# A fused two-layer graph transformer on one core: the second layer's work moved one group later, with its x2 turned over by way of DRAM

## The reference

```python
# layer 0 (8 heads of 32)
nx = ln(x, ln1_g, ln1_b)
q, k, v = heads(nx @ wq + bq), heads(nx @ wk + bk), heads(nx @ wv + bv)
scores = q @ k.T / sqrt(32) + where(adj > 0, 0.1 * adj * adj, -inf)
x1 = x + (softmax(scores) @ v) @ wo + bo
x2 = x1 + gelu(ln(x1, ln2_g, ln2_b) @ w1 + b1) @ w2 + b2      # hidden size 1024
# layer 1 (one head of 256)
sc = where(adj == 0, -inf, (x2 @ Wq) @ (x2 @ Wk).T / sqrt(256))
y = x2 + (softmax(sc) @ (x2 @ Wv)) @ Wo + bo
out = layer_norm(y) * gamma + beta
```

## Time and profile before

| | |
|---|---|
| time, median of 3 | 890.98 us (890.16 to 891.61) |
| profiled execution | 891.15 us, its span 889.4 us |
| PE busy | 853.3 us (96%) |
| PEld busy | 754.3 us (85%) |
| DVE busy | 703.3 us (79%) |
| ACT busy | 609.6 us (69%) |
| POOL busy | 507.5 us (57%) |
| DMA moved | 107.32 MB, mean 121 GB/s |
| mean granted TensorE clock | 0.983 |

### The profile page before, as it was taken

One profiled execution on the slowest core, in us unless ns is written; L12 is line 12 of the kernel. 1 busy time (PEld: TensorE's weight loads), 2 busy tenths in 40 slices (PEclk: granted clock), 3 DMA queues, 4 the chain that ended last, 5 costly groups with the idle time before them and its releaser, 6 DMA issues.

```text
span 889.4 us, 21938 instructions
## 1 busy us (share of the span) xinstructions
PE 853.3 (96%) x7059; PEld 754.3 (85%) x7059; DVE 703.3 (79%) x2548; ACT 609.6 (69%) x1830; POOL 507.5 (57%) x374
## 2 busy tenths in 40 slices
PE   8899797799999999999999999999999999999996
PEld 8787687589898989889898988989798988989795
DVE  6695777868888898888888797888889887875636
ACT  5684865667868676776768676786867677684542
POOL 3522743756666565775647566666656577655312
PEclk9899999799999999999999999999999999999998
DMA  8000245445536353444546343553635343343001
GB/s 272 16 24 13 66 105 187 129 152 136 177 94 200 101 180 99 127 154 114 181 118 189 106 146 105 138 176 95 200 96 182 86 124 120 99 143 115 24 1 36
DMA packets 131122, 107.32 MB, mean 121 GB/s; under 512 B 5750, under 2 KB 112908, under 8 KB 131084
## 3 DMA queue, kind: packets, MB, share of 16 engines
q1 hardware_dynamic: 131068, 106.85, 40.5%
q10 hardware_dynamic: 16, 0.00, 0.0%
HBM read 61.48 MB, written 45.35 MB: 120 GB/s over the span
## 4 chain that ended last, share of the span: by engine, by line
PE 74%; ACT 3%; DVE 3%; POOL 1%; issue 1%; DVEq 0%; POOLq 0%
PE bank L455 21%; PE bank L457 20%; PE bank L456 20%; PE bank L618 3%; PE bank L743 3%; PE bank L774 3%; PE bank L642 3%; ACT p L1116 2%; PE bank L724 1%; DVE p L1540 1%; PE bank L767 0%; POOL p_s L2013 0%; POOL x_bo L1983 0%; POOL x_b L1993 0%; DVE stats L1375 0%
## 5 line engine op out<-in xcount | busy, mean ns | idle before, releaser
L1052 ACT ACTIVATE p_s<-bank,neg_max 128x128 f32<-128x128 f32 x464 | 163.0, 391 | 78.2 <-DVE neg_max L1443 78.1
L2013 POOL TENSOR_TENSOR p_s<-p_s,rsum 128x512 f32<-128x512 f32 x116 | 118.1, 1041 | 73.9 <-DVE rsum L1450 52.2
L455 PE MATMUL bank<-w_hi,hT_hi 128*128 128x256 f32 x512 | 147.5, 288 | 1.3 <-DVE hT_lo L1316 1.3
L457 PE MATMUL bank<-w_hi,hT_lo 128*128 128x256 f32 x512 | 144.1, 281 | 0.0
L456 PE MATMUL bank<-w_lo,hT_hi 128*128 128x256 f32 x512 | 144.0, 281 | 0.0
L1443 DVE CUSTOM_DVE_ANT_0 bank<-bank,bias 128x128 f32<-128x128 f32 x464 | 117.4, 325 | 2.0 <-PE bank L618 1.5
L455 PE MATMUL bank<-n2T_hi,w_hi 128*128 128x512 f32 (+1 forms) x272 | 111.4, 409 | 5.1 <-DVE hT_lo L1316 5.1
L1083 ACT ACTIVATE bank<-bank,vec_cols 128x512 f32<-128x512 f32 (+1 forms) x136 | 86.5, 636 | 31.1 <-PE bank L457 22.5
L1052 ACT ACTIVATION_READ_ACCUMULATOR p_s<-bank,neg_max 128x1 f32 x464 | 107.1, 231 | 0.0
L456 PE MATMUL bank<-n2T_lo,w_hi 128*128 128x512 f32 (+1 forms) x272 | 105.2, 387 | 0.0
L457 PE MATMUL bank<-n2T_hi,w_lo 128*128 128x512 f32 (+1 forms) x272 | 105.1, 387 | 0.0
(11 more groups left out here) (242 smaller groups left out, 2432.6 us busy)
## 6 DMA issues: line engine op xcount, KB each, us to landing
parked<-pT SPq DMA_DIRECT2D x116, 256.0 KB, 3.8
pT<-parked SPq DMA_DIRECT2D x15, 1024.0 KB, 5.5
p_s<-parked SPq DMA_DIRECT2D x14, 1024.0 KB, 7.7
xs<-in_x SPq DMA_DIRECT2D x15, 512.0 KB, 3.9
out<-y SPq DMA_DIRECT2D x14, 512.0 KB, 3.0
x_bo<-in_x SPq DMA_DIRECT2D x13, 512.0 KB, 3.8
parked_x<-nx SPq DMA_DIRECT2D x48, 128.0 KB, 2.5
hT_hi<-parked_x SPq DMA_DIRECT2D x12, 512.0 KB, 5.0
```

Of the source, the lines that this page charges most:

```text
L455: mm(out, a_hi, b_hi, start=first, stop=False)
L457: return mm(out, a_lo, b_hi, start=False, stop=last)
L1052: last = run(to, of, ACT.Exp, scale=-1.0, bias=neg_max[:, r, place:place + 1], accum_out=psum[:, r, place:place + 1])
L2013: P.tensor_tensor(p_s[:, r, :, :], p_s[:, r, :, :], rsum[:, r, :, None].to_broadcast([128, 4, NODES]), ALU.mult).then_inc(pool_p, 1)
```

## The change

Layer 1 of a group is made one turn later. A turn has a new name `gl = gp - 3` for the group of layer 1, and `gc` becomes `gp - 4`. Turn 4 has neither (`None`). `last_turn` makes layer 1 of group 14 among the up-projections of group 15. `late(g)` is true for groups 2 to 14.

For these groups x2 is no longer transposed by TensorE: VectorE transposes blocks of x2 into x1_b2's place (`x2blocks`), SP stores them (`store_x2T`, four DMAs of 128 KB) and loads them (`load_x2T`, one DMA of 512 KB); in the next turn ScalarE makes the high part (`landed_high`) and VectorE the low part (`x2T_low`). x2 plus bo1 is stored to DRAM (`store_x2`, 512 KB) and loaded into y's place (`load_y`, 512 KB); `residual3` adds to it there. The mask of layer 1 is made from a second load of the adjacency (`load_adj1`, 256 KB, `mask_landed`), and `move_up` is gone from the turns. On TensorE the q-k product stands ahead of the values of gp, and the scores ahead of both value-output products.

```diff
 SP
+            def load_x2T(g):
+                sp.wait_ge(x2T_store, 64 * g - 64)
+                sp.wait_ge(pe_s1, g)
+                sp.dma_start(x2T_f[:, :, :], parked_x2T[g].rearrange("t c j a b i -> (c j) t (a b i)")).then_inc(x2T_load, 16)
+            def load_y(g):
+                sp.wait_ge(x2_store, 16 * g - 16)
+                sp.wait_ge(out_store, 16 * g)
+                sp.dma_start(y[:, :, :].rearrange("p b d -> p (b d)"), parked_x2[g]).then_inc(y_load, 16)
...
-            def turn(gp, gc):
+            def turn(gp, gb, gl, gc):
...
                     load_adj(gp + 1)
-                store(gc)
+                load_adj1(gb)
+                if gc is not None:
+                    store(gc)
                 store_blocks(gp, 0)
+                if gl is not None:
+                    load_y(gl)
                 if not is_last(gp):
                     load_nx(gp + 1)
+                store_x2T(gb)
                 load_xbo(gp)
                 if not is_last(gp):
                     store_blocks(gp, 1)
+                load_x2T(gb)
                 for q in pairs(gp):
                     load_blocks(gp, q)
+                store_x2(gb)
 TensorE
@@ n2_transpose
-                    pe.wait_ge(act_t, g)
-                    pe.wait_ge(dve_t, g)
-                    pe.wait_ge(dve_s1, g)
+                    done = g if opening(g, 3) else g - 1
+                    pe.wait_ge(act_t, done)
+                    pe.wait_ge(dve_t, done)
+                    pe.wait_ge(dve_s1, done)
@@ turn
                 mlp_down(gb, 0)
+                if gl is None:
+                    out_project(ga, 0)
                 mlp_down(gb, 1, (0,))
                 if size(gp) > 2:
                     scores(gp, 1)
+                if gl is None:
+                    out_project(ga, 1)
+                    mlp_down(gb, 1, (1,))
+                    project_v(gp, 0)
+                    n2_transpose(ga, True)
+                    project_v(gp, 1)
+                    return
                 mlp_down(gb, 1, (1,))
                 out_project(ga, 0)
-                x2_transpose(gb)
                 out_project(ga, 1)
+                t_project(gl)
                 project_v(gp, 0)
-                t_project(gb)
-                vo_project(gb, 0, True)
-                scores1(gb)
-                vo_project(gb, 1, True)
+                scores1(gl)
+                vo_project(gl, 0, True)
+                vo_project(gl, 1, True)
                 n2_transpose(ga, True)
-                p1_transpose(gb)
+                p1_transpose(gl)
@@ last_turn
-                for j in range(4):
-                    mlp_up(gb, j, True)
+                mlp_up(gb, 0, True)
+                mlp_up(gb, 1, True)
+                t_project(gl)
+                mlp_up(gb, 2, True)
+                mlp_up(gb, 3, True)
+                scores1(gl)
+                vo_project(gl, 0, False)
+                attend(ga, 0)
                 mlp_up(gb, 4, True)
-                attend(ga, 0)
+                vo_project(gl, 1, False)
                 mlp_up(gb, 5, True)
                 mlp_up(gb, 6, True)
+                pe.wait_ge(dve_vo, gl)
                 out_project(ga, 0)
                 mlp_up(gb, 7, True)
+                p1_transpose(gl)
                 mlp_down(gb, 0)
+                attend1_pairs(gl)
+                mlp_down(gb, 1, (0,))
                 n2_transpose(ga, False)
-                mlp_down(gb, 1)
+                mlp_down(gb, 1, (1,))
 ScalarE
+            def landed_high(g):
+                act.wait_ge(x2T_load, 16 * g - 16)
+                act.wait_ge(pe_vo, pair0(g))
+                for t in range(KT):
+                    identity(nx_split(x2T[0], g, t), x2_landed(g, t)).then_inc(act_x2T_hi, 1)
@@ turn
                 nx_high(gp)
+                if gl is not None:
+                    landed_high(gl)
                 for j in range(4):
                     gelu(gb, j)
...
                 if whole:
-                    exps(gp, 1, 0)
-                    exps(gp, 1, 1)
-                for t in range(KT):
-                    x2T_copy(gb, (t,))
-                    x2T_high(gb, (t,))
-                if whole:
-                    exps(gp, 1, 2)
-                    exps(gp, 1, 3)
+                    for r in range(HPT):
+                        exps(gp, 1, r)
+                if gl is not None:
+                    t_copy(gl)
                 v_copy(gp, 0)
-                t_copy(gb)
-                vo_copy(gb)
-                exps1(gb)
+                if gl is not None:
+                    vo_copy(gl)
+                    exps1(gl)
@@ last_turn: landed_high(gl) ahead of the GELUs; between GELU 5 and 6 a probe for Exp, exps1(gl), a probe for Gelu
 VectorE
+            def x2blocks(g):
+                dve.wait_ge(dve_x2, pair0(g) + 2)
+                turned = flat(x1_b2[:, :, :]).rearrange("p (t c b i) -> p t b c i", t=KT, c=4, b=PER)
+                for t in range(KT):
+                    V.transpose(turned[:, t], x2[:, :, 128 * t:128 * t + 128].rearrange(
+                        "p b (c j) -> p b c j", c=4)).then_inc(dve_x2blocks, 1)
@@ x2T_low
+                    if late(g):
+                        V.tensor_tensor(nx_split(x2T[1], g, t), x2_landed(g, t), nx_split(x2T[0], g, t).bitcast(f32),
+                                        ALU.subtract).then_inc(dve_x2T, 1)
+                        continue
@@ turn
-                norm3(gc)
+                if gc is not None:
+                    norm3(gc)
+                if gl is not None:
+                    x2T_low(gl)
                 attn_low(ga, 0)
...
                 residual1(ga, 0, True)
-                x2T_low(gb)
+                x2blocks(gb)
                 residual1(ga, 1, True)
                 sums2(ga, 0)
+                if gl is not None:
+                    t_copy(gl)
                 sums2(ga, 1)
...
                     blocks(gp, 1, 0)
-                t_copy(gb)
...
-                biased1(gb)
+                if gl is not None:
+                    biased1(gl)
...
-                vo_copy(gb)
+                if gl is not None:
+                    vo_copy(gl)
...
-                inverse_sums1(gb)
-                residual3(gb, 0)
-                residual3(gb, 1)
+                if gl is not None:
+                    inverse_sums1(gl)
+                    residual3(gl, 0)
+                    residual3(gl, 1)
 GpSimd
+            def mask_landed(g):
+                k = size(g)
+                pool.wait_ge(adj1_load, 16 * g - 16)
+                pool.wait_ge(dve_s1, g)
+                pool.sem_inc(stand_pool, 1)
+                P.tensor_copy(pen1[:, 0:k, :], adj_w[:, 0:k, :]).then_inc(pool_adj_f, 1)
...
+                P.tensor_scalar(pen1[:, 0:k, :], pen1[:, 0:k, :], 0.0, MASKED, ALU.is_equal, ALU.mult).then_inc(pool_pen1, 1)
@@ first_turn: move_up(2) is gone; second_turn: mask1(2) and move_up(3) are gone
@@ turn
                 for r in range(HPT):
                     normal(gp, 0, r)
-                x2_plus_bo(gb)
...
                 if size(gp) > 2:
                     normal(gp, 1, 3)
+                x2_plus_bo(gb)
                 x_plus_bo(gp)
                 x1_plus_b2(ga)
-                mask1(ga)
-                move_up(gp)
+                mask_landed(gb)
```

More of the change, by code:

```diff
@@ L54, in is_last, with late, opening @@
     return isinstance(g, int) and g == GROUPS - 1
+def late(g):
+    return not (isinstance(g, int) and (g < 2 or g > GROUPS - 3))
+def opening(g, first):
+    return isinstance(g, int) and g < first
 def toks(g):
@@ L590, in project_v @@
                 elif not (isinstance(g, int) and g < 3):
-                    pe.wait_ge(*((dve_x1, pair0(g) - 1), (dve_vo, g - 2))[q])
+                    pe.wait_ge(*((dve_x1, pair0(g) - 1), (dve_vo, 1 if opening(g, 4) else g - 3))[q])
+                    if q == 1 and not opening(g, 4):
+                        pe.wait_ge(dve_x1, pair0(g))
                 for b in (2 * q, 2 * q + 1):
@@ L730, in t_project @@
                     pe.wait_ge(dve_s1, g)
+                elif isinstance(g, int) and g == GROUPS - 3:
+                    pe.wait_ge(act_p, 4 * pair0(g + 2) + 4)
+                elif late(g):
+                    pe.wait_ge(dve_x2, pair0(g + 2))
                 for m in range(KT):
@@ L742, in scores1 @@
                     for t in range(KT):
-                        last = mm(bank[at("s1", g)][:, nodes(b)], home("tT", g)[:, t, nodes(b)], home("x2T_f", g)[:, t, nodes(b)],
+                        x = x2_landed(g, t)[:, b] if late(g) else home("x2T_f", g)[:, t, nodes(b)]
+                        last = mm(bank[at("s1", g)][:, nodes(b)], home("tT", g)[:, t, nodes(b)], x,
                                   start=(t == 0), stop=(t == KT - 1))
@@ L1554, in residual3 @@
                     dve.wait_ge(dve_r1, g + 1)
-                    dve.wait_ge(pool_x2b, g + 1)
-                    if not is_last(g):
```

(28 more changed lines are left out.)

204 lines of the change are left out of this document (138 added, 66 removed).

## The result

The changed kernel takes 942.05 us (median of 5 runs, 941.21 to 944.40), the kernel before 891.18 us beside it. The ratio is 1.058, its 95% interval 1.0565 to 1.0592: slower by 51 us. The forecast was 946 in a range of 905 to 961.

A forecast was written before the change was run, and what follows sets the result against it. TensorE's queue of work was taken to bound the kernel. Eleven turns of 3.0 + 0.5 + 0.5 = 4.0 us make 44, the ends 11.3, together 55.3 on 891.15 us: 946, range 905 to 961.

The forecast's parts named there:

- The head: Start of a turn: late x2T load delays ScalarE's first GELU and TensorE's up-projections, +3.0 us a turn.
- The clock: TensorE's granted clock falls behind new waits of 2.3 and 1 us: between 0 and 1.7 us a turn, 0.5 taken.
- Rival C: The clock falls in every turn at the full price, 11 x 1.2 us more, 959; chance 0.06.
- The tail: End of a turn: VectorE's masked scores hold back TensorE's relief and a GpSimd lock delays VectorE, +0.5 us a turn.
- a tail without a lock: Tail if VectorE's x2T low copies don't contend with GpSimd's gain: n2 slightly earlier, -0.15 us a turn.
- the first runs, then the gain, then the second: Behind norm3, GpSimd's 2.38 us gain runs between VectorE's two x2T low copies, making VectorE 1.65 us late at avT_lo.
- 3.0 + 0.5 + 0.5: Price of turns 5 to 15: late load at the start, VectorE's chain at the end, slower clock; 4.0 us a turn.
- The ends: Second turn -0.9, turn 4 -2.0 and +1.0 clock, turn 5 +1.7, last turn +10, turn 16 +1.5: 11.3 us.
- B: Faster: TensorE's relief of 1.1 us a turn arrives if masked scores and load are in time, 885; chance 0.06.
- A: x2T load lands in time or its wait is absorbed; 0.6 head and 0.5 tail a turn, 913; chance 0.16.
- D: Neither cost nor gain: delays and relief are taken up in VectorE's idle fifth, 891; chance 0.02.

The follow-up runs named there:

- Experiments 1 to 3: Changed kernel with one edit each: x2T load ahead of stores, 899.56 us; high copies behind GELUs, 899.27 us; key projections between fourth and fifth up-projection, 908.50 us.
- kernel 1: Changed kernel with the load of x2T issued on SP ahead of the four stores of the second half of the blocks: 899.56 us, ratio 1.0105.
- Experiments 4 to 7: Old tail order on the changed kernel, 929.72 us; with early load, 889.24; with early load, only VectorE's tT copy moved, 895.54, only TensorE's and ScalarE's order, 921.67.
- kernels 5 and 11: Changed kernel with early x2T load and old tail order, 889.24 us; the same plus key projections after the fourth up-projection and turn 4's chain brought forward, 885.73 us.
- kernel 5: Changed kernel with both repairs, the x2T load ahead of the block stores and the old order in the tail: 889.24 us, ratio 0.9997.
- kernel 4: Changed kernel with the old tail order on TensorE, ScalarE and VectorE, the x2T load left late: 929.72 us, ratio 1.0448.
- kernel 7: Changed kernel with early x2T load and the old order on TensorE and ScalarE, VectorE's tT copy kept between the statistics: 921.67 us, ratio 1.0364.

## Why the prediction held, and where it did not

**The head.** The mechanism is as forecast, and each step of it: issue at the turn's start, landing at +5.1 (forecast +4.7), ScalarE's GELU late, fifth up-projection at +8.32 (+8.1). Experiments 1 to 3 show it from three sides. The size of the wait was 2.5 us a turn, not 3.0: the eighth up-projection did not wait for VectorE at +13.05, since the slow clock brought TensorE there only at +14.2 by itself. Taking the late load away gives back 37.3 us in ten turns, 3.73 a turn; I had 3.0 and a share of the clock.

**The clock.** Too small: 0.5 forecast, 1.38 measured. Rival C's mechanism, a fall in every turn, was the true one: each of the ten turns has a mean granted clock of 0.97. It did not give 959 since the head and the tail were cheaper.

**The tail.** This term failed: +0.5 forecast, -0.1 measured. TensorE has 1.12 us a turn less to do (507.91 us in before's ten turns, 496.67 in kernel 1) and waits 1.02 us ahead of n2. That is close to the -0.15 that the prediction gave for a tail without a lock. In kernel 1 the 0.2 us left in the head take up the rest, so its period is before's (50.86 against 50.87).

The step that failed is "the first runs, then the gain, then the second", which put +0.65 on the tail. x2T's low copies took 1.28 us together, not over 2, and GpSimd's gain gave way, 3.35 us instead of the 2.38 of the earlier trace rows:

```profile
452.94 1.28 DVE L1654 TENSOR_TENSOR x2T_lo<-x2T_f,x2T_hi 128x512 fp32r<-128x512 f32 x2
455.36 0.69 DVE L1431 TENSOR_TENSOR avT_lo<-bank,avT_hi 128x512 fp32r<-128x512 f32 x1 [1.14 <-ACT avT_hi L1082]
...
453.10 3.35 POOL L2173 TENSOR_TENSOR y<-y,gamma_r 128x1024 f32<-128x1024 f32 x1 [1.61 <-DVE y L1507]
```

VectorE still waits 1.14 us behind it, so nothing is late. That one of the two stands still while the other works is what the Trainium skill states in "SBUF — State Buffer", section "Who interferes with whom", and this row agrees with it (3.35 is 2.38 and about what was left of the pair). The same section gives the ports to the one that issues first; by that GpSimd, from 453.10 on, would have gone ahead of VectorE's second copy, as the prediction had it, and the row shows otherwise.

The rest of the tail held as forecast: the statistics end at 476.47 and the masked scores begin at 480.84, 4.4 us later (4.5), and TensorE idles 1.02 us ahead of n2 (1.0). What the prediction did not ask is whether the relief could be had by another order. Experiments 4 to 7 show that the wait came from the new order. Without it 0.88 of the 1.1 us arrives.

**What adds up.** By TensorE's own rows, per steady turn: wait in the head +2.52, wait ahead of n2 +1.02, clock +1.38, less work -1.12, and 0.08 that it idled before: +3.72, measured +3.71. The forecast was 3.0 + 0.5 + 0.5. Terms of opposite sign made 40 for ten turns and 37.1 measured look closer than its parts were; that is luck.

By the kernels: the late load +3.73, the order +0.87, the delay by a group with both repaired -0.88. These are differences along one row of kernels, so that they add up is no test. Taken the other way round, the old order is worth 1.37 (kernel 4) and the early load 3.23. The two overlap by 0.5 us, most of it the clock.

**The ends.** Turn 4 -2.05 (forecast -1.0), turn 5 +3.03 (+5.7), turn 16 +3.49 (+1.5: the clock fell there too, 0.97), the last turn +11.20 (+10), in kernels 5 and 11 +9.8: TensorE's added work, busy 67.97 us after 56.98. Up to turn 4 it was -2.8 where I had -0.9; most of this is the scatter of the opening, and the second turn itself gave 0.5. So about 2 of the 5 us by which the total of 50.0 is under the 55.3 are scatter.

**Rivals.** B's point was at VectorE's masked scores and the load, and kernel 5 shows it to be the right one: with both in time TensorE's relief arrives. But B's -13 us for 12 turns was too much, it is 0.88 a turn, so with the ends even a repaired change is even with before. A (load in time, 913) has kernel 1 as its test: 900, because its 0.5 us in the tail are not there, and its 0.6 in the head are 0.35, which the relief pays for. D is out.

**Open.** The mean price of the clock is 0.92 us a turn behind the wait in the head alone (kernel 4: 506.23 us of work, kernel 5 with the same order: 497.00) and 0.42 behind a wait as long ahead of n2 (kernel 7: 501.24). Turn by turn it is not a smaller price but a rarer one. Two turns of kernel 4, then two of kernel 7:

```profile
374.94:428.74 53.80, 51.10 (x418) 44.96 (x416) 44.74 (x158) 35.41 (x110) 33.35 (x24) 0.97 0.61 175
322.17:374.94 52.77, 50.06 (x418) 43.66 (x416) 44.74 (x158) 35.18 (x109) 33.34 (x24) 1.00 0.62 179
```

```profile
532.47:586.18 53.71, 51.12 (x418) 45.31 (x416) 44.69 (x158) 35.44 (x109) 35.17 (x25) 0.97 0.60 181
586.18:638.01 51.83, 49.42 (x417) 43.79 (x416) 44.22 (x158) 35.33 (x109) 31.67 (x23) 1.00 0.60 177
```

The clock is 0.97 in all ten turns of the changed kernel, in six of kernel 4 and in four of kernel 7. In each of these turns TensorE's work takes 51.0 to 51.1 us, 1.3 more than the 49.7 to 49.8 of a steady turn of kernels 1 and 5. At full clock it takes 49.5 to 50.1 us in kernel 4 and 49.3 to 49.7 in kernel 7. In kernel 1, with 1.02 us ahead of n2 and 0.2 in the head, it never falls. What decides whether it falls behind a wait of 2.4 us, no run here tells.

## What to carry to other kernels

When data is parked and fetched a turn later, its load must stand in the queue ahead of transfers that wait for late work, and the engine that uses it first must not have its own critical work queued behind that use; look at both queues, since either alone repairs it. Before an order on TensorE is changed, check which slot on the next engine the new result falls into: a copy at the start of a chain over three engines costs its wait and its length, while in the chain's idle time it costs VectorE nothing. Move the two together: the copy's slot alone gained only 0.45 of the 0.87 us. A software pipeline one stage deeper pays per turn and is charged at the end: in kernel 5 the ten steady turns gained 8.8 us, and the last turn alone cost 9.8.

## What was not expected of the hardware

- Two VectorE instructions with both inputs in SBUF, one behind the other, went through together (1.28 us) while GpSimd's instruction, which began 0.16 us behind the first, took 3.35 us instead of 2.38; in the head, where GpSimd's 2.40 us instruction had begun first (486.13), VectorE's pair from 487.95 took 2.14.
- The same idle time of 2.4 us of TensorE, once a turn, brought the clock down in six turns of ten at one place and in four at another. Where it fell, TensorE's work took 1.3 us more than in a turn of kernel 5, both times.
- DMA traffic rose from 136 to 170 GB/s in the steady turns, and to 186 in kernel 5, and TensorE waited for a parked block ahead of attention only once in either, by 1.0 and 0.9 us (before: once, by 1.5). The cover over the added transfers held.
